# Routing on VectorE: the best two of a group as the largest of seven pair sums, and group differences in another order

## What is computed

```
x = x + 0.5 * ffn(layernorm(x))
x = x + attn(layernorm(x))          # a gated convolution with a linear recurrence
x = x + 0.5 * ffn(layernorm(x))
```

```
scores = sigmoid(tokens @ router_weight.T)          # 32 experts
sfc = scores + router_bias
grp = sfc.reshape(T, 4, 8)                          # 4 groups of 8 experts
group_scores = top_k(grp, 2)[0].sum(-1)             # the sum of the best two of a group
gidx = top_k(group_scores, 2)                       # the two best groups
tmp = where(expert is in a chosen group, sfc, 0)
topk_idx = top_k(tmp, 4)
topk_w = scores[topk_idx] / (their sum + 1e-20) * 2.5
```

## Time and profile before

| | |
|---|---|
| median of 3 runs | 672.98 us (671.9 to 673.3) |
| the profiled execution | 672.07 us |
| its span, first to last instruction | 670.3 us |
| TensorE (PE) busy | 98% |
| VectorE (DVE) busy | 82% |
| GpSimd (POOL) busy | 67% |
| ScalarE (ACT) busy | 63% |
| granted TensorE clock | 1.000 of full speed |

### The profile page before, as it was taken

The page is one execution under the profiler, slowest core; times in us unless marked ns, Lnnn a source line. Parts: engine busy times, 40 slices in busy tenths (PEclk is TensorE's granted clock), DMA queues, the critical chain, the costliest instruction groups (busy, mean ns, idle before and its releaser), DMA issues. The chain is left out here.

```text
span 670.3 us, 10334 instructions
## 1 busy us (share of the span) xinstructions
PE 656.8 (98%) x3083; PEld 530.8 (79%) x3083; DVE 548.9 (82%) x1540; ACT 420.7 (63%) x804; POOL 446.5 (67%) x452
## 2 busy tenths in 40 slices
PE   8899999999999999999999999999999999999997
PEld 7787888888888887888888888888878778777675
DVE  5888889979878877879879898788979868867765
ACT  4756666675676656766476755767676566655554
POOL 2346667866776766766677775867676776776564
PEclk9999999999999999999999999999999999999999
DMA  9664909248091925629084470917419074380561
GB/s 223 144 142 99 188 11 226 51 110 162 26 224 42 215 53 124 133 80 206 17 187 101 108 147 22 227 41 168 104 32 223 2 172 100 75 181 17 118 137 32
DMA packets 60232, 78.30 MB, mean 117 GB/s; under 512 B 8176, under 2 KB 27664, under 8 KB 60176
## 3 DMA queue, kind: packets, MB, share of 16 engines
q1 hardware_dynamic: 59600, 77.63, 52.2%
q10 hardware_dynamic: 576, 0.02, 0.1%
HBM read 74.49 MB, written 3.15 MB: 116 GB/s over the span
## 5 line engine op out<-in xcount | busy, mean ns | idle before, releaser
L576 POOL TENSOR_TENSOR hid_lo<-hid,hid_hi 128x512 fp32r<-128x512 f32 x270 | 348.3, 1294 | 188.3 <-ACT hid_hi L689 188.0
L840 DVE TENSOR_TENSOR weighted<-gate_ps,raw 128x512 f32<-128x512 f32 x256 | 175.2, 684 | 69.7 <-ACT gate_ps L681 64.1
L681 ACT ACTIVATE gate_ps<-gate_ps 128x512 f32<-128x512 f32 x256 | 148.7, 581 | 119.7 <-PE gate_ps L1119 116.4
L689 ACT ACTIVATE hid_hi<-hid 128x512 fp32r<-128x512 f32 x272 | 170.4, 626 | 64.4 <-DVE hid L853 61.1
L853 DVE TENSOR_TENSOR hid<-weighted,up_ps 128x512 f32<-128x512 f32 x256 | 174.3, 681 | 8.0 <-issue 0.5
L1190 PE MATMUL down_ps<-hid_lo,wt_hi 128*128 128x512 f32 x272 | 108.0, 397 | 0.2 <-DVE hid_lo L861 0.2
L1187 PE MATMUL down_ps<-hid_hi,wt_hi 128*128 128x512 f32 x272 | 107.8, 396 | 0.0
L1188 PE MATMUL down_ps<-hid_hi,wt_lo 128*128 128x512 f32 x272 | 107.7, 396 | 0.0
L1117 PE MATMUL gate_ps<-xT_hi,wt_hi 128*128 128x512 f32 x170 | 72.0, 423 | 0.0
L1117 PE MATMUL up_ps<-xT_hi,wt_hi 128*128 128x512 f32 x170 | 68.4, 402 | 2.4 <-DVE hid L853 2.3
L1118 PE MATMUL gate_ps<-xT_lo,wt_hi 128*128 128x512 f32 x170 | 67.3, 396 | 0.0
(11 more groups left out here) (187 smaller groups left out, 1108.4 us busy)
## 6 DMA issues: line engine op xcount, KB each, us to landing
raw<-wT_hbm SPq DMA_DIRECT2D x96, 512.0 KB, 11.6
raw<-wT_hbm SPq DMA_DIRECT2D x62, 256.0 KB, 4.5
x_ln<-in_L_attn_x SPq DMA_DIRECT2D x8, 256.0 KB, 4.0
x_res<-in_L_attn_x SPq DMA_DIRECT2D x8, 256.0 KB, 3.7
out_x<-x SPq DMA_DIRECT2D x7, 256.0 KB, 2.3
raw<-in_L_ffn_gate_w SPq DMA_DIRECT2D x4, 256.0 KB, 4.9
raw<-in_L_ffn_up_w SPq DMA_DIRECT2D x4, 256.0 KB, 4.9
raw<-in_L_ffn_down_w SPq DMA_DIRECT2D x4, 256.0 KB, 5.2
```

What stands on the lines that cost most here:

```text
L576: nc.gpsimd.tensor_tensor(hid_lo[s][:, :], hid[s][:, :], hid_hi[s][:, :].bitcast(F32), ALU.subtract)\
L681: nc.scalar.activation(bank[:, :] if j else silu_sb[:, :], bank[:, :], ACT.Silu).then_inc(silu_done, 1)
L689: nc.scalar.activation(hid_hi[s][:, :], hid[s][:, :], ACT.Copy).then_inc(hid_hi_done, 1)
L840: V.tensor_tensor(weighted[j % 2][:, :], gate_ps[n % BANKS][:, :], wb[:, j - 1, :], ALU.mult)\
```

## The change

Steps 5 to 13 become steps 5 to 10. The 8 scores of a group are halved: the sums of elements i and i + 4 (4 pair sums) and their maxima (4 values), then the same with the four maxima (2 sums, 2 maxima), then the last sum. The largest of the 7 pair sums is the sum of the best two. For this `biased` is now a tile in SBUF, no longer in PSUM. Step 11 copies gsum with its two dimensions swapped, the difference (step 12) and the comparison (13) run with the compared group as the outermost dimension, and beat_at has the token tile as a further dimension. Steps 6 and 8 no longer wait for the step before. The chain has 24 steps, spread over the same slots.

```diff
-        beat_at = sb("beat_at", [P, NG, NG])
+        beat_at = sb("beat_at", [P, NG, TT, NG])
...
-        biased = routed[:, 128:256].rearrange("p (t e) -> p t e", t=TT)
...
+        biased = sb("biased", [P, TT, E])
+        HALF, QUARTER = PG // 2, PG // 4
+        PAIRS = HALF + QUARTER + 1
+        pair_sum = sb("pair_sum", [P, TT * NG, PG])
+        top_half = sb("top_half", [P, TT * NG, HALF])
+        top_quarter = sb("top_quarter", [P, TT * NG, QUARTER])
         gsum = sb("gsum", [P, TT, NG])
...
+        gsum_by_group = sb("gsum_by_group", [P, NG, TT])
+        gdiff = routed[:, 256:320].rearrange("p (h x) -> p h x", h=NG)
+        beats = routed[:, 320:384].rearrange("p (h x) -> p h x", h=NG)
...
-        ROUTE = 26
+        ROUTE = 24
...
-                st.wait()
+                if n not in (6, 8):
+                    st.wait()
...
                 elif n == 5:
-                    st.done(V.tensor_reduce(per_group(best1), by_group(biased), AX.X, ALU.max))
+                    st.done(V.tensor_tensor(pair_sum[:, :, 0:HALF], grouped(biased)[:, :, 0:HALF],
+                                            grouped(biased)[:, :, HALF:PG], ALU.add))
                 elif n == 6:
-                    st.done(V.tensor_tensor(by_group(is_best), by_group(biased), over_group(best1), ALU.is_equal))
+                    st.done(V.tensor_tensor(top_half[:, :, :], grouped(biased)[:, :, 0:HALF],
+                                            grouped(biased)[:, :, HALF:PG], ALU.max))
                 elif n == 7:
-                    st.done(V.scalar_tensor_tensor(others[:, :, :], is_best[:, :, :], FAR, biased[:, :, :],
-                                                   ALU.mult, ALU.add))
+                    st.done(V.tensor_tensor(pair_sum[:, :, HALF:HALF + QUARTER], top_half[:, :, 0:QUARTER],
+                                            top_half[:, :, QUARTER:HALF], ALU.add))
                 elif n == 8:
-                    st.done(V.tensor_reduce(per_group(n_best), by_group(is_best), AX.X, ALU.add))
+                    st.done(V.tensor_tensor(top_quarter[:, :, :], top_half[:, :, 0:QUARTER],
+                                            top_half[:, :, QUARTER:HALF], ALU.max))
                 elif n == 9:
-                    st.done(V.tensor_reduce(per_group(best_other), by_group(others), AX.X, ALU.max))
+                    st.done(V.tensor_tensor(pair_sum[:, :, PAIRS - 1], top_quarter[:, :, 0], top_quarter[:, :, 1],
+                                            ALU.add))
                 elif n == 10:
-                    st.done(V.tensor_scalar(far_single[:, :], n_best[:, :], 1.5, FAR, ALU.is_lt, ALU.mult))
+                    st.done(V.tensor_reduce(gsum[:, :, :].rearrange("p t g -> p (t g)"), pair_sum[:, :, 0:PAIRS],
+                                            AX.X, ALU.max))
                 elif n == 11:
-                    st.done(V.tensor_tensor(best1_tied[:, :], far_single[:, :], best1[:, :], ALU.add))
+                    st.done(V.tensor_copy(gsum_by_group[:, :, :], gsum[:, :, :].rearrange("p t g -> p g t")))
                 elif n == 12:
-                    st.done(V.tensor_tensor(best2[:, :], best1_tied[:, :], best_other[:, :], ALU.max))
+                    st.done(V.tensor_tensor(gdiff.rearrange("p h (t g) -> p h t g", t=TT),
+                                            gsum_by_group[:, :, :].unsqueeze(3).broadcast_to([P, NG, TT, NG]),
+                                            gsum[:, :, :].unsqueeze(1).broadcast_to([P, NG, TT, NG]),
+                                            ALU.subtract))
                 elif n == 13:
-                    st.done(V.tensor_tensor(gsum[:, :, :].rearrange("p t g -> p (t g)"), best1[:, :], best2[:, :],
-                                            ALU.add))
+                    st.done(V.tensor_tensor(routed[:, 320:384], routed[:, 256:320],
+                                            beat_at[:, :, :, :].rearrange("p h t g -> p (h t g)"), ALU.is_ge))
                 elif n == 14:
-                    st.done(V.tensor_tensor(gdiff[:, :, :].rearrange("p t (g h) -> p t g h", g=NG),
-                                            gsum[:, :, :].unsqueeze(2).broadcast_to([P, TT, NG, NG]),
-                                            gsum[:, :, :].unsqueeze(3).broadcast_to([P, TT, NG, NG]),
-                                            ALU.subtract))
+                    st.done(V.tensor_reduce(grank[:, :], beats.rearrange("p h x -> p x h"), AX.X, ALU.add))
```

More of the change, by code:

```diff
@@ L225, in macaron_kernel @@
         score = routed[:, 0:128].rearrange("p (t e) -> p t e", t=TT)
-        biased = routed[:, 128:256].rearrange("p (t e) -> p t e", t=TT)
[L227 to L234, removed]
+        biased = sb("biased", [P, TT, E])
[4 more added lines that the diff above has]
+        top_quarter = sb("top_quarter", [P, TT * NG, QUARTER])
         gsum = sb("gsum", [P, TT, NG])
-        gdiff = routed[:, 256:320].rearrange("p (t x) -> p t x", t=TT)
-        beats = routed[:, 320:384].rearrange("p (x h) -> p x h", h=NG)
+        gsum_by_group = sb("gsum_by_group", [P, NG, TT])
+        gdiff = routed[:, 256:320].rearrange("p (h x) -> p h x", h=NG)
+        beats = routed[:, 320:384].rearrange("p (h x) -> p h x", h=NG)
         grank = routed[:, 452:452 + TT * NG]
@@ L650, in _ @@
             const.done(nc.gpsimd.affine_select(
-                out=beat_at[:, :, :], in_=zeros[:, 0:NG * NG].rearrange("p (g h) -> p g h", g=NG),
-                fill=1e-37, compare_op=ALU.is_gt, base=0, pattern=[[1, NG], [-1, NG]], channel_multiplier=0))
+                out=beat_at[:, :, :, :],
+                in_=zeros[:, 0:NG * TT * NG].rearrange("p (h t g) -> p h t g", h=NG, t=TT),
+                fill=1e-37, compare_op=ALU.is_gt, base=0, pattern=[[-1, NG], [0, TT], [1, NG]],
+                channel_multiplier=0))
             for q in range(EARLY):
@@ L879, in xT_low, with grouped @@
                  .then_inc(xT_lo_done[k], 1)
[L882 to L886, removed]
+            def grouped(t):
+                return t[:, :, :].rearrange("p t (g c) -> p (t g) c", g=NG)
             def over_group(t):
-                return per_group(t).unsqueeze(3).broadcast_to([P, TT, NG, PG])
+                return t[:, :].rearrange("p (t g) -> p t g", t=TT).unsqueeze(3).broadcast_to([P, TT, NG, PG])
             def route_step(k, b, st, n):
@@ L934, in route_step @@
                 elif n == 15:
-                    st.done(V.tensor_tensor(routed[:, 320:384].rearrange("p (t x) -> p t x", t=TT), gdiff[:, :, :],
-                                            beat_at[:, :, :].rearrange("p g h -> p (g h)").unsqueeze(1)
-                                            .broadcast_to([P, TT, NG * NG]), ALU.is_ge))
+                    st.done(V.tensor_scalar(gmask[:, :], grank[:, :], float(GTOP), -1.0, ALU.is_lt, ALU.mult))
                 elif n == 16:
[L939 to L942, removed]
@@ L946, in route_step @@
                         over_group(gmask), ALU.bitwise_and))
-                elif n == 19:
+                elif n == 17:
                     V.memset(hold[:, 5:6], 0.0)
@@ L951, in route_step @@
                     st.done(last)
-                elif n == 20:
+                elif n == 18:
                     st.done(V.memset(top8[:, :, TOP:8], FAR))
-                elif n == 21:
+                elif n == 19:
                     V.memset(hold[:, 6:7], 0.0)
@@ L958, in route_step @@
                     st.done(last)
-                elif n == 22:
+                elif n == 20:
                     st.done(V.scalar_tensor_tensor(chosen[:, :, 0:E], replaced[:, :, 0:E], (FAR + GONE) / 2,
                                                    score[:, :, :], ALU.is_lt, ALU.mult))
+                elif n == 21:
+                    st.done(V.tensor_reduce(wsum[:, :], chosen[:, :, :], AX.X, ALU.add))
+                elif n == 22:
+                    st.done(V.reciprocal(winv[:, :], wsum[:, :]))
                 elif n == 23:
[L963 to L966, removed]
                     st.done(V.scalar_tensor_tensor(w_tok[:, :, :].rearrange("p e t -> p t e"), chosen[:, :, 0:E], SCALE,
```

## The result

| | kernel before | changed kernel |
|---|---|---|
| median | 672.98 us (671.79 to 673.47, 5 runs) | 684.12 us (681.12 to 684.17, 5 runs) |
| ratio to before | | 1.0163 (95% interval 1.0141 to 1.0186) |
| profiled execution / its span | 672.07 / 670.3 us | 684.17 / 682.4 us |
| mean granted TensorE clock | 1.000 | 0.997 (1.000 in the run of 681.12 us) |

What follows compares the result with a forecast made beforehand. TensorE, busy 98%, was taken as the bound, so VectorE work counts only where TensorE waits. 672.07 - 0.95 (first chain) + 4.0 (four middle units) + 0 (three units) + 9.6 (eight others) = 684.7, said as 685 us, range 675 to 698.

Steps and rivals of the forecast that it cites:

- Two SBUF inputs as the cause: L930's stretched times: a VectorE step with both inputs in SBUF waits for GpSimd; the change adds six such steps.
- The plain saving of 0.68 us: Per routing chain, undisturbed: nine removed steps take 2.11 us, the seven added 1.43, saving 0.68 us.
- The copy: Step 11, SBUF to SBUF: counted as waiting at full price; without its wait the chain is 0.44 us shorter.
- 0.44 us for each of seven: Price per wait in seven new waiting steps: 3.1 us, less 0.68 saved, 2.4 us more VectorE time a chain.
- The start, -0.95: First chain (block 0), GpSimd idle: 2.47 us becomes 1.5, and TensorE gets w_tok 0.95 us earlier.
- (a): Four middle units of the second FFN: late hidden tiles stall TensorE 1.0 us each, +4.0 (1.6 to 6).
- my case of 0.4 a unit: Middle second-FFN units if VectorE beats GpSimd at step 5: steps 6, 7 and 12 collide, stall 0.4 us.
- (b): Three units of the first FFN: VectorE's idle time takes in the added 2.4 us, 0 (up to 1).
- (c): Other eight units with a chain, four at the beginning, four at the end: 1.2 us each, +9.6 (2.4 to 19).
- 1 (nothing contends): Rival: no step waits for GpSimd, only the plain saving is left, 670 us; chance 0.08.
- 2 (slack takes it all): Rival: steps wait for GpSimd, but VectorE's idle time absorbs it, 673 to 674 us; chance 0.10.
- 3 (in step with GpSimd, 702 us): Rival: chain locks in step with GpSimd, costing 3 us rather than 1 in twelve units, 702 us; chance 0.15.

Runs made afterwards that it cites:

- experiment 1: The kernel before with only biased moved from PSUM to SBUF, all 26 steps kept: 683.61 us, ratio 1.0175.
- 4: The kernel before with gsum also written to PSUM, so L930's difference reads one operand from each memory: 670.38 us, ratio 0.9979.
- 3: The changed kernel with no chain step having two SBUF inputs, three more instructions a chain: 669.73 us, ratio 0.9970.
- experiment 6: The changed kernel with gmask alone in PSUM, so only the mask is free: 680.05 us, ratio 1.0119.
- experiment 7: The changed kernel with the copy of gsum moved by half a slot, ahead of hid of tile 6, beside unit (4,4): 680.93 us, ratio 1.0134.
- experiment 8: The changed kernel with the waits of steps 6 and 8 put back: 685.13 us, ratio 1.0197.

## Why the prediction was right, step by step

- **What bounds the kernel.** Right. TensorE's busy share goes only from 98 to 97%, and nearly all of the loss is TensorE waiting for VectorE's results, plus a stretch of slow clock behind one such wait.
- **Two SBUF inputs as the cause.** Right, and shown: by experiment 1 (one operand moved, three lines stretch), by 4 (double broadcast without conflict, no stretch) and by 3 (none left, all constant). One sentence of the working was too broad: not every other step reads an operand from PSUM. L917 and L919 read SBUF alone, but one tile each, and match_replace (L957) names two SBUF tiles; the trace shows it as a load of 8 values and then an instruction over 36 elements, which is constant at 177 to 184 ns.
- **The plain saving of 0.68 us.** Right. The shortest of L908, L914, L920 and L926 are 215, 169, 172 and 158 ns against estimates of 220, 190, 170 and 170.
- **The copy.** I counted it with a full price. It does wait, in 7 of 16 blocks (0.91 us at 628.84, ending 0.03 behind GpSimd), but in the middle units of the second FFN it slips by just ahead of GpSimd, and the difference behind it pays 1.0. As the pair was counted as two, the sum hardly suffers.
- **0.44 us for each of seven.** Too high. By the groups, steps 5 to 9 and the copy have 38.5 us together where 16 x 1.16 = 18.6 would do, the mask 7.7 more than its 4.6 before, the difference 4.0 more than its 10.2: 31.6 us, 2.1 a chain, not 3.1. VectorE's added time is 1.3 us a chain rather than 2.4. L908, L911, L917, L920 and L926 have medians within 0.03 us of their shortest, and the difference and the mask carry nearly half of the waiting time, with L914 next: whether a step waits is set by its slot, alike in all middle units, and a mean taken from one line at one slot doesn't carry over.
- **The start, -0.95.** Right: w_tok's transpose starts at 19.59 instead of 20.50, 0.91 earlier. In unit (1,0) as a whole 0.83 us of it is left.
- **(a) Four middle units, +4.0 (1.6 to 6).** Too low: 6.5. VectorE won the first race, steps 6, 7 and 12 collided as in my case of 0.4 a unit, and the hidden tile cost 0.4 to 0.5, yet the unit lost 1.64. The difference then delayed the add of ffn 1 and with it TensorE's use of `side`, 0.7 us, and another 0.35 further on. I had looked at hidden tiles only, not at who else stands in VectorE's queue behind the chain.
- **(b) Three units of the first FFN, 0.** Right: -0.24, +0.16, +0.14.
- **(c) The others, +9.6 (2.4 to 19).** 6.6, inside (0.1 of it for unit (1,0), the first chain's gain aside), but not evenly: five of the eight lie within 0.25 us of before, and one has 3.6. Of that, 1.5 us are the slow clock, for which the sum had no term. What the Trainium skill says of this conflict ("SBUF — State Buffer", section "Who interferes with whom": an exclusive lock, so that one engine waits until the other has ended) agrees with the trace: L928 at 447.15 ends some 0.1 us behind GpSimd. It gave the sign; the size came from places.
- **Sum.** 12.7 forecast, 12.1 between the profiled executions. The mechanism was right; that the size agrees so well is luck. The price of a wait was too high by half, (a) missed 2.5 us on one side and (c) 3.0 on the other, and 1.5 us came from a clock that nobody had counted.
- **The rivals.** 1 (nothing contends) fell with experiments 1 and 4. 2 (slack takes it all) holds, to within 0.24 us, for the three units of (b) and for (1,3), (1,7), (4,5), (4,6), not for the kernel. 3 (in step with GpSimd, 702 us) didn't come about: beside the chain of unit (4,3) GpSimd was idle 0.2 to 1.5 us between its instructions.

## What to carry to other kernels

Where GpSimd streams from SBUF, a VectorE instruction with both inputs in SBUF, however small, can take as long as GpSimd's instruction: compare its shortest and its median duration, and put one of its inputs in PSUM. Fewer and shorter instructions are no gain if they buy this; here three lines with one moved operand cost as much as the whole change, and the same algorithm with one operand of each step in PSUM gained 0.3%, of which 0.2% are to be had in the kernel before by moving one operand of one line. When adding delay to a queue, ask for everything behind it, not only for the main loop's tiles.

## What was not expected of the hardware

- The end of the wait has a fixed form: where it waited, an instruction over 16, 32, 64 and 128 elements ended 0.05, 0.05 to 0.06, 0.09 and 0.15 us behind GpSimd's end (L920, L914, L928 and L940, in 5, 10, 11 and 12 of 16 blocks), the copy of 16 elements 0.03 behind. The lag grows with the elements, as if the instruction began to stream only then; no run shows that directly.
- `scalar_tensor_tensor` waits like `tensor_tensor` (L914 in experiment 1, 837 ns), and so does a copy from SBUF to SBUF over 16 elements (L926).
- Not every GpSimd instruction is in the way. Those over 512 elements are (hid_lo, y_lo and x alike), but the power of 4 elements (rstd) takes 1.01 us, and a copy that runs in the middle of it takes its 0.17 us, here and in experiments 6, 7 and 8. Why isn't shown.

```profile
124.11 1.01 POOL L585 TENSOR_TENSOR rstd<-var_eps,neg_half 128x4 f32<-128x4 f32 x1
...
124.86 0.17 DVE L926 COPY gsum_by_group<-gsum 128x16 f32<-128x16 f32 x1
```

- TensorE's granted clock fell to its lower level for some 3.4 us after it had stood still for 2.1 us, in a stretch where it had been busy before. The other two profiles with this stall show it too (experiment 6 for some 6.8 us, experiment 8 for 3.4); after 0.88 us (experiment 7) it didn't fall, nor after the 1.0 and 1.15 us waits at 611 and 634 us. Four of five runs of the changed kernel have the lower mean clock, and it takes 1.5 us in the profiled one (8 products 0.43 apart instead of 0.23).
